# Values of the attention in runs of four key tiles, row sums ahead of the second run, maxima spread anew

## The chip, the cores and the metric

The kernel runs on one core of a Trainium2 chip. Its engines are TensorE (PE in the profile, PEld for its weight loads), VectorE (DVE), ScalarE (ACT), GpSimd (POOL) and SyncE (SP, which here only issues transfers). They run side by side, each through its own list of instructions, and meet at semaphores. The metric is the time of the whole program on the device in microseconds (us), as the median of several runs.

## The reference

Two layers over x, 16 batches of 1024 nodes with 256 channels, each with a residual and a layer norm. The change touches the attention of the first one:

```python
g = relu(einsum('bcn,bnm->bcm', fea, adj * A_s) * para)     # q, from a weighted adjacency
q = g.T in 4 heads of 64;  k, v = (x @ kv_w) in 4 heads of 64
attn = softmax(einsum('bhnd,bhmd->bhnm', q, k) * scale, axis=-1)
out = einsum('bhnm,bhmd->bhnd', attn, v)
x = layernorm(x + out)
```

The second layer aggregates over the adjacency and has two linear layers with batch norms. It comes after the first and is not touched.

## The kernel before

`attention_layer` goes through 16 batches (`over_batches`: batch 0, a loop for 1 to 14, batch 15). In a batch TensorE first does `g_product` (96 matmuls into `sc_ps`), then the products for k and v with the maxima of head 0 between them, and then the four heads.

Scores are computed transposed: a *tile* of 128 keys against 1024 queries, so a head has 8 tiles. Each tile takes two pieces of 512 queries, and each piece two matmuls into the same place of `sc_ps` (L834): one of `qa`, `ka` and one of `qb`, `kb`. The low parts of q lie in `qb`, and with them one row with the negative maximum of every query. So the first `qb` matmul of a head can't begin before that row has arrived. ACT takes the exponential of a whole tile (L378) into `probs`, a ring of 4 tiles. `sc_ps` has two places, so tile i waits for the exponential of tile i-2.

The *values* of a tile (L850) multiply `probs` by v into `pv_ps`; the profile counts 4 matmuls a tile. They free the tile's place in `probs`. In code, tiles come in 4 pairs p = 0 to 3. The values of a pair follow after the scores of the next one, the last pair's after pair 0 of the next head. I call values that stand together a *run*.

The *maxima* of head h+1 are made during head h: 16 *halves* (8 query tiles times two pieces of 512 keys), each one matmul (L803) into one of the two banks of `mx_ps` and one DVE reduction (L562). `MAX_HALVES[h][p][k]` says how many halves stand ahead of unit k of pair p, the last number how many behind the last unit; a unit is the work on a piece (in pair 0, on the parts of a tile). When all 16 are reduced and merged (L566), TensorE transposes the result (L812), DVE negates it into `row` (L573), and SP sends it into `qb` (L192, `store_row`). The next head waits for it (`row_in`).

The *row sums* of head h-1: POOL adds the first seven tiles in six additions (L303), DVE the last one (`add_last`, L579). TensorE sums over the partitions (`sum_up`, L860), ACT copies the result out (`den_copy`, L392), TensorE transposes it (`transpose_sums`, L868), and DVE inverts it (`invert_sums`, L585). The head's output goes by ACT (`head_copy`, L386), TensorE (`transpose_back`, L876) and DVE (`add_head`, L597) into `res`.

During head 3, `prepare` does the first steps of the next batch: TensorE transposes x in two halves (L714, pairs 0 and 1) and makes the k product behind the scores of pair 2 (L698); ACT copies xT_high (L315), DVE makes xT_low (L513). ACT has in its list, behind the exponentials of each pair, also w_high (L338), distance (L325), tanh (L332) and the k copies (L343). In head 0 it normalises the previous batch (L398) behind pairs 0 and 1.

## Time and profile before

| | us |
|---|---|
| median of 3 runs | 2834.18 (2833.53 to 2835.38) |
| the profiled run | 2833.73 |
| its span in the trace | 2831.4 |
| TensorE busy | 2694.5 (95%) |
| DVE busy | 1993.4 (70%) |
| ACT busy | 1668.6 (59%) |
| POOL busy | 1284.4 (45%) |

The attention layer lies between about 20 and 1951 us of the span. Start times in the timeline are counted from the start of the span. Starts of matmuls are measured, their ends are modelled: in a stream of matmuls one is shown as busy for 0.39 us although the next starts 0.23 us later, so a short wait of TensorE can hide in its busy time. The distance from start to start tells more.

### The profile page before, as it was taken

What the parts mean: (1) busy time and instruction counts of PE and PEld (TensorE: products, weight loads), DVE (VectorE), ACT (ScalarE), POOL (GpSimd) and SP (SyncE); (2) the same over time, 40 slices, a digit from 0 to 9 for tenths busy, and PEclk for the clock granted to TensorE, in tenths of its full rate; (3) what the DMA queues carried; (4) which work ended last, traced back from release to release, by engine and by line L of the source; (5) the groups of instructions that cost most, each with busy time, mean ns of one, the idle gap of its engine ahead of it and who ended that gap; (6) DMA issues with size and microseconds to landing.
All of it is one profiled execution on the core that took longest, in us unless ns stands there. A gap on an engine that the chain in (4) does not pass through costs nothing. (4 is left out here: it accounts for less than half of the span.)

```text
span 2831.4 us, 39434 instructions
## 1 busy us (share of the span) xinstructions
PE 2694.5 (95%) x12436; PEld 1857.6 (66%) x12436; DVE 1993.4 (70%) x2875; ACT 1668.6 (59%) x2162; POOL 1284.4 (45%) x684
## 2 busy tenths in 40 slices
PE   7999999999999999999999999996799999989964
PEld 5565665656656566675666756563688888878854
DVE  6687786877878788796887868773533333348878
ACT  7567576765767666676675767654322222237768
POOL 3755657566475754757557575655100000000025
PEclk9999999999999999999999999998899999999976
DMA  4232222233222332222322222222222223215566
GB/s 138 60 94 94 74 67 85 71 100 89 67 71 78 100 93 67 74 78 74 98 88 74 67 85 76 83 65 87 77 90 89 95 104 112 89 30 185 185 237 253
DMA packets 126943, 272.01 MB, mean 96 GB/s; under 512 B 11952, under 2 KB 62128, under 8 KB 123312
## 3 DMA queue, kind: packets, MB, share of 16 engines
q1 hardware_dynamic: 126896, 271.42, 29.7%
q8 instruction: 25, 0.41, 0.1%
q14 instruction: 22, 0.18, 0.0%
HBM read 178.79 MB, written 62.98 MB: 85 GB/s over the span
## 5 line engine op out<-in xcount | busy, mean ns | idle before, releaser
L303 POOL TENSOR_TENSOR psum<-psum,probs 128x1024 f32<-128x1024 f32 x320 | 784.9, 2453 | 144.2 <-ACT probs L378 118.2
L378 ACT ACTIVATE probs<-sc_ps 128x1024 f32<-128x1024 f32 x512 | 508.7, 1024 | 410.0 <-PE sc_ps L834 360.6
L562 DVE TENSOR_REDUCE mx<-mx_ps 128x1 f32<-128x512 f32 x768 | 519.7, 690 | 276.0 <-PE mx_ps L803 274.1
L850 PE MATMUL pv_ps<-probs,v 128*64 128x512 f32 x2048 | 492.4, 604 | 0.0
L834 PE MATMUL sc_ps<-qa,ka 128*128 128x512 f32 x1024 | 387.0, 403 | 0.0
L834 PE MATMUL sc_ps<-qb,kb 128*128 128x512 f32 x1024 | 380.8, 395 | 0.4
L803 PE MATMUL mx_ps<-ka,qa 128*128 128x512 f32 x768 | 315.9, 425 | 10.1 <-DVE mx L562 2.9
L850 PEld LDWEIGHTS pv_ps<-probs,v 128*64 128x64 f32 x2048 | 125.6, 136 | 224.8 <-issue 194.1
L1184 DVE TENSOR_TENSOR agg_lo<-ag_ps,agg_hi 128x1024 fp32r<-128x1024 f32 x32 | 39.2, 1225 | 312.0 <-ACT agg_hi L1111 312.0
L803 PEld LDWEIGHTS mx_ps<-ka,qa 128*128 128x128 f32 x768 | 139.7, 187 | 179.8 <-issue 77.9
L834 PEld LDWEIGHTS sc_ps<-qa,ka 128*128 128x128 f32 x1024 | 187.6, 188 | 105.3 <-issue 64.1
L1080 POOL TENSOR_TENSOR rstd<-veps,neg_half_b 128x4 f32<-128x4 f32 x1 | 1.0, 1007 | 515.9 <-DVE veps L1200 515.9
L526 DVE TENSOR_TENSOR w_lo<-scr,w_hi 128x1024 fp32r<-128x1024 f32 x128 | 224.0, 1750 | 5.3 <-ACT w_hi L338 5.1
L521 DVE SCALAR_TENSOR_TENSOR scr<-scr,adj_ring 128x1024 f32<-128x1024 f32 x128 | 222.8, 1741 | 3.8 <-ACT scr L332 2.8
L834 PEld LDWEIGHTS sc_ps<-qb,kb 128*128 128x128 f32 x1024 | 191.0, 188 | 47.3 <-issue 6.0
L303 POOL TENSOR_TENSOR psum<-probs 128x1024 f32<-128x1024 f32 x64 | 152.5, 2383 | 148.7 <-ACT probs L378 148.6
L1111 ACT ACTIVATE agg_hi<-ag_ps 128x1024 fp32r<-128x1024 f32 x32 | 32.9, 1029 | 311.7 <-PE ag_ps L1272 300.6
L767 PE MATMUL sc_ps<-w_hi,x_hi 128*128 128x512 f32 x512 | 207.1, 405 | 6.8 <-DVE w_lo L526 6.8
L767 PE MATMUL sc_ps<-w_lo,x_hi 128*128 128x512 f32 x512 | 200.6, 392 | 0.0
L767 PE MATMUL sc_ps<-w_hi,x_lo 128*128 128x512 f32 x512 | 200.0, 391 | 0.0
L267 POOL TENSOR_TENSOR rstd<-veps,neg_half 128x8 f32<-128x8 f32 x16 | 32.4, 2025 | 349.5 <-DVE veps L52 349.5
L283 POOL TENSOR_TENSOR qb<-scr,qa 64x1024 fp32r<-64x1024 f32 x64 | 153.4, 2396 | 74.1 <-ACT scr L360 69.2
(197 smaller groups left out, 5554.3 us busy)
## 6 DMA issues: line engine op xcount, KB each, us to landing
adj_ring<-in_adj_dram SPq DMA_DIRECT2D x128, 512.0 KB, 3.7
pre_scratch<-pre SPq DMA_DIRECT2D x28, 1024.0 KB, 4.5
pre<-pre_scratch SPq DMA_DIRECT2D x28, 1024.0 KB, 4.9
x<-in_x_dram SPq DMA_DIRECT2D x16, 1024.0 KB, 5.6
kb<-ka SPq DMA_DIRECT2D x64, 256.0 KB, 3.1
res<-in_x_dram SPq DMA_DIRECT2D x16, 1024.0 KB, 5.6
x_scratch<-res SPq DMA_DIRECT2D x16, 1024.0 KB, 4.5
x1s<-x_scratch SPq DMA_DIRECT2D x16, 1024.0 KB, 7.5
```

The lines of the kernel that those rows point to most:

```text
L283: pool.tensor_tensor(qb[h][own(h), :], scr[own(h), h // 2, :], qa[h][own(h), :].bitcast(F32), ALU.subtract).then_inc(s["ql_done"], 1)
L303: pool.tensor_tensor(psum[:, h % 2, :], probs[:, 0, :] if k == 1 else psum[:, h % 2, :], probs[:, k % PR, :], ALU.add).then_inc(s["pool_ad ...
L378: nc.scalar.activation(probs[:, i % PR, :], sc_ps[:, t % 2, :], ACT.Exp, scale=SCALE)\
L521: nc.vector.scalar_tensor_tensor(d, d, -1.0, adj_ring[:, n % AR, :], ALU.add, ALU.mult)\
L526: nc.vector.tensor_tensor(w_lo[:, n % WR, :], scr[:, n % DR, :], w_hi[:, n % WR, :].bitcast(F32), ALU.subtract).then_inc(s["wlo_done"], 1)
L562: nc.vector.tensor_reduce(mx2[:, nh, n:n + 1], mx_ps[:, nh, :], AX.X, ALU.max)\
L767: ins = nc.tensor.matmul(sc_ps[:, c, cols], lhsT, rhs, start=n == 0 and k == 0, stop=n == T - 1 and k == 2)
L803: nc.tensor.matmul(out, qa[h][:, n * P:(n + 1) * P], ka[h][:, nh * BANK:(nh + 1) * BANK], start=True, stop=True).then_inc(s["mx_ready"], 1)
L834: ins = nc.tensor.matmul(sc_ps[:, t % 2, cols], k[:, keys], q[:, cols], start=part == 0, stop=part == 1)
L850: ins = nc.tensor.matmul(pv_ps[nh * HD:(nh + 1) * HD, h % 2, :], v[:, i, h * HD:(h + 1) * HD], probs[:, i % PR, nh * BANK:(nh + 1) * BANK] ...
L1111: nc.scalar.activation(agg_hi[:, :, j * BANK:(j + 1) * BANK], ag_ps[:, j, :, :], ACT.Copy)\
L1184: nc.vector.tensor_tensor(agg_lo[:, :, cols], ag_ps[:, j, :, :], agg_hi[:, :, cols].bitcast(F32), ALU.subtract)\
```

## The change

The values of a head now come in two runs of four tiles. The first run (tiles 0 to 3) stands behind the scores of pair 2, the second (tiles 4 to 7) behind the scores of pair 0 of the next head, for head 3 at the end of the batch. `sum_up` of the previous head moves from pair 1 to pair 2, directly ahead of the first run, `transpose_sums` directly behind that run, and `transpose_back` stays in pair 3, where no values follow any more. ACT's `den_copy` stays behind pair 1, DVE's `add_last` moves from behind two maxima halves to behind four. `MAX_HALVES` is written anew: no unit has two halves ahead of it except at the start of head 0; head 0 has six halves in pair 2 and three in pair 3, heads 1 and 2 have 4, 5, 5 and 2 (before 4, 4, 6 and 2). No work is added or removed.

```diff
--- before.py
+++ after.py
@@ -65,9 +65,10 @@
     SG = P // 4
     SN = N // 4
     SQ = SN // P
-    MAX_HALVES = [[[0, 2, 1], [2, 1, 1, 1, 0], [2, 1, 1, 1, 1], [1, 1, 0, 0, 0]]] + \
-        2 * [[[0, 1, 1, 1, 1], [1, 1, 1, 1, 0], [2, 1, 1, 1, 1], [1, 1, 0, 0, 0]]]
-    SUM_PAIR, DEN_PAIR, BACK_PAIR = 1, 2, 3
+    MAX_HALVES = [[[0, 2, 1], [0, 1, 1, 1, 1], [1, 1, 1, 1, 2], [1, 1, 1, 0, 0]]] + \
+        2 * [[[0, 1, 1, 1, 1], [1, 1, 1, 1, 1], [1, 1, 1, 1, 1], [1, 1, 0, 0, 0]]]
+    OLD_PAIR, NEW_PAIR = 0, 2
+    GROUP = T // 2
     POOL_ADDS = T - 2
 
     x_v = x.rearrange("b (p t) c -> b p t c", t=T)
@@ -472,7 +473,7 @@
                             prepare(b + 1, h, p)
                         if h and p == 0:
                             head_copy(b, h - 1)
-                        if h and p == SUM_PAIR:
+                        if h and p == NEW_PAIR - 1:
                             den_copy(b, h - 1)
 
             x_high(0, range(T))
@@ -641,10 +642,9 @@
                 maxima_row(b, 1)
 
                 for h in (1, 2):
-                    maxima(b, h + 1, range(0, 1))
+                    maxima(b, h + 1, range(0, 2))
                     add_last(b, h - 1)
-                    maxima(b, h + 1, range(1, 4))
-                    maxima(b, h + 1, range(4, 7))
+                    maxima(b, h + 1, range(2, 7))
                     invert_sums(b, h - 1)
                     maxima(b, h + 1, range(7, T))
                     maxima_row(b, h + 1)
@@ -919,24 +919,24 @@
                             maxes(p, k)
                             scores(b, h, n, parts, part_halves)
                         maxes(p, len(units))
-                        if h and p == DEN_PAIR:
-                            transpose_sums(b, h - 1)
                         if more and p == PAIRS - 1:
                             transpose_maxima(b, h + 1)
-                        if h and p == BACK_PAIR:
+                        if h and p == PAIRS - 1:
                             transpose_back(b, h - 1)
                         if not last:
                             prepare(b + 1, h, p)
-                        if h and p == SUM_PAIR:
-                            sum_up(b, h - 1)
-                        if p:
-                            values(b, h, i - 2)
-                            values(b, h, i - 1)
-                        elif h:
-                            values(b, h - 1, T - 2)
-                            values(b, h - 1, T - 1)
-                values(b, HEADS - 1, T - 2)
-                values(b, HEADS - 1, T - 1)
+                        if h and p == OLD_PAIR:
+                            for n in range(GROUP, T):
+                                values(b, h - 1, n)
+                        if p == NEW_PAIR:
+                            if h:
+                                sum_up(b, h - 1)
+                            for n in range(GROUP):
+                                values(b, h, n)
+                            if h:
+                                transpose_sums(b, h - 1)
+                for n in range(GROUP, T):
+                    values(b, HEADS - 1, n)
 
             pe.wait_ge(s["ident_set"], 3)
             transpose_x(0, 0)
```

How this moves TensorE's list, first at the end of head 1 and the start of head 2 (`ka2`, `qa2` belong to head 2, `ka3`, `qa3` to the maxima of head 3). Before:

```order
L812 MATMUL mx_ps<-ident,mxs 8x128 [waits merged]
L876 MATMUL pv_ps<-ident,heads_t 128x128 [waits rden_done]
L876 MATMUL pv_ps<-ident,heads_t 128x128 x3
L850 MATMUL pv_ps<-probs,v 64x512 [waits exp_done]
L850 MATMUL pv_ps<-probs,v 64x512
L850 MATMUL pv_ps<-probs,v 64x512 [waits exp_done]
L850 MATMUL pv_ps<-probs,v 64x512
L834 MATMUL sc_ps<-qa2,ka2 128x512 [waits kl_done,qa_in2,exp_done]
L834 MATMUL sc_ps<-qa2,ka2 128x512
```

The same place now, down to the first `qb` matmul:

```order
L812 MATMUL mx_ps<-ident,mxs 8x128 [waits merged]
L876 MATMUL pv_ps<-ident,heads_t 128x128 [waits rden_done]
L876 MATMUL pv_ps<-ident,heads_t 128x128 x3
L834 MATMUL sc_ps<-qa2,ka2 128x512 [waits kl_done,qa_in2,exp_done]
L834 MATMUL sc_ps<-qa2,ka2 128x512
L803 MATMUL mx_ps<-ka3,qa3 128x512 [waits kl_done,qa_in3,row_done]
L834 MATMUL sc_ps<-qa2,ka2 128x512 [waits exp_done]
L834 MATMUL sc_ps<-qa2,ka2 128x512
L803 MATMUL mx_ps<-ka3,qa3 128x512
L834 MATMUL sc_ps<-qb2,kb0 128x512 [waits ql_done,kb_in0,row_in]
```

The values of two tiles between the transposes and the scores have gone behind the scores of pair 0; the rest of the order is the same in both.

Second, TensorE in head 3 from the second half of the x transposes (L714) to the k product (L698). Before:

```order
L714 MATMUL mx_ps<-ident,x32 128x128 x7
L860 MATMUL pv_ps<-psum,ones_a 32x256 [waits copied_out,acc_done]
L860 MATMUL pv_ps<-psum,ones_a 32x256 x3
L850 MATMUL pv_ps<-probs,v 64x512 [waits res_added,exp_done]
...
L834 MATMUL sc_ps<-qa3,ka3 128x512 [waits exp_done]
...
L868 MATMUL pv_ps<-ident,heads_t 128x128 [waits den_copied]
L868 MATMUL pv_ps<-ident,heads_t 128x128
L698 MATMUL mx_ps<-xT_hi,kvw_hi 128x512 [waits row_done,xtl_done]
```

Now:

```order
L714 MATMUL mx_ps<-ident,x32 128x128 x7
L834 MATMUL sc_ps<-qa3,ka3 128x512 [waits exp_done]
...
L834 MATMUL sc_ps<-qa3,ka3 128x512 [waits exp_done]
...
L698 MATMUL mx_ps<-xT_hi,kvw_hi 128x512 [waits row_done,xtl_done]
```

Only the scores of pair 2, eight matmuls, are left between them. The row sums, the values and the sums' transposes have moved behind the k product.

## Rows read from the trace of the kernel before

**Rows 1.** Busy time by stretch: engines with their instruction counts, granted clock, DMA share, GB/s

```profile
core 0: us, PE busy (x) PEld busy (x) DVE busy (x) ACT busy (x) POOL busy (x), PEclk, DMA share, GB/s
50.00:1950.00 1900.00, 1887.73 (x8905) 1194.80 (x8904) 1504.26 (x2260) 1268.54 (x1596) 1193.49 (x493) 1.00 0.26 78
```

**Rows 2.** The page's costliest groups: busy us, mean ns of one, idle before, releaser

```profile
L303 POOL TENSOR_TENSOR psum<-psum,probs 128x1024 f32<-128x1024 f32 x320 | 784.9, 2453 | 144.2 <-ACT probs L378 118.2
...
L562 DVE TENSOR_REDUCE mx<-mx_ps 128x1 f32<-128x512 f32 x768 | 519.7, 690 | 276.0 <-PE mx_ps L803 274.1
```

**Rows 3.** Timeline (start us, us, engine, line): runs of two tiles, of four; head copy

```profile
1910.44 0.40 PE L803 MATMUL mx_ps<-ka,qa 128*128 128x512 f32 x1
1910.77 1.94 PE L850 MATMUL pv_ps<-probs,v 128*64 128x512 f32 x8
1912.64 0.50 PE L803 MATMUL mx_ps<-ka,qa 128*128 128x512 f32 x1
1912.97 0.39 PE L834 MATMUL sc_ps<-qa,ka 128*128 128x512 f32 x1
...
1915.28 0.39 PE L834 MATMUL sc_ps<-qb,kb 128*128 128x512 f32 x1
...
1912.75 0.60 ACT L386 ACTIVATE heads_t<-pv_ps 128x512 f32<-128x512 f32 x1 [0.87 <-PE pv_ps L850]
...
1828.38 3.65 PE L850 MATMUL pv_ps<-probs,v 128*64 128x512 f32 x16
1831.96 0.50 PE L767 MATMUL sc_ps<-w_hi,x_hi 128*128 128x512 f32 x1
```

**Rows 4.** Timeline, the row's way into head 0: batch 14, then batch 15

```profile
1745.98 0.27 PE L812 MATMUL sc_ps<-ident,mxs 128*8 128x128 f32 x1
...
1746.29 0.28 DVE L573 TENSOR_SCALAR row<-sc_ps 8x128 fp32r<-8x128 f32 x1 [0.37 <-PE sc_ps L812]
...
1746.59 0.70 SPq L192 DMA_DIRECT2D qb<-row  x1
...
1747.52 1.08 PE L834 MATMUL sc_ps<-qa,ka 128*128 128x512 f32 x4
1748.63 0.70 PE L834 MATMUL sc_ps<-qb,kb 128*128 128x512 f32 x2
...
1866.26 0.27 PE L812 MATMUL sc_ps<-ident,mxs 128*8 128x128 f32 x1
...
1866.87 0.70 SPq L192 DMA_DIRECT2D qb<-row  x1
...
1868.72 0.30 PEld L834 LDWEIGHTS sc_ps<-qb,kb 128*128 128x128 f32 x2 [0.27 <-DMA qb<-row]
```

**Rows 5.** Timeline of TensorE, batch 14: sums' transposes; end of head 1 to head 2

```profile
1780.69 0.38 PE L868 MATMUL pv_ps<-ident,heads_t 128*128 128x128 f32 x2
1781.00 1.94 PE L850 MATMUL pv_ps<-probs,v 128*64 128x512 f32 x8
...
1785.27 0.27 PE L812 MATMUL mx_ps<-ident,mxs 128*8 128x128 f32 x1
...
1789.27 0.63 PE L834 MATMUL sc_ps<-qb,kb 128*128 128x512 f32 x2
```

**Rows 6.** Timeline, head 0 of batch 14: an exponential; head 1 begins

```profile
1753.48 1.03 ACT L378 ACTIVATE probs<-sc_ps 128x1024 f32<-128x1024 f32 x1
...
1766.65 0.73 PE L834 MATMUL sc_ps<-qa,ka 128*128 128x512 f32 x2
```

**Rows 7.** Timeline, head 3 of batch 14: x transposes, xT_low, exponentials, k product

```profile
1815.60 1.03 PE L714 MATMUL mx_ps<-ident,x 128*128 128x128 f32 x8
...
1821.10 0.47 PE L698 MATMUL mx_ps<-xT_hi,kvw_hi 128*128 128x512 f32 x1
...
1817.85 1.23 DVE L513 TENSOR_TENSOR xT_lo<-mx_ps,xT_hi 128x1024 fp32r<-128x1024 f32 x1 [1.72 <-ACT xT_hi L315]
...
1820.32 1.95 ACT L378 ACTIVATE probs<-sc_ps 128x1024 f32<-128x1024 f32 x2 [1.28 <-PE sc_ps L834]
...
1827.31 1.94 ACT L378 ACTIVATE probs<-sc_ps 128x1024 f32<-128x1024 f32 x2
```

**Rows 8.** Busy time by stretch, the end of the attention layer; columns as in rows 1

```profile
1947.00:1951.00 4.00, 1.97 (x17) 0.71 (x14) 1.43 (x2) 0.98 (x2) 0.39 (x1) 1.00 0.00 0
```

## The prediction

> **What bounds the kernel now.** First the busy time by stretch: from 50 to 1950 us, the attention layer, TensorE is busy 1887.7 of 1900 us at a granted clock of 1.00, its full 2.4 GHz, while ACT, DVE and POOL have 21 to 37% to spare [rows 1]. Nothing is changed behind it. So the question is how long TensorE's own list of work takes there, and where it begins to wait. A batch takes 120.3 us: the same transfer is issued at 1746.59 and 1866.87 [rows 4].
>
> Second, TensorE's timeline around a run of values. Ten 512-column matmuls for scores and maxima in a row take 2.31 us (1912.97 to 1915.28) [rows 3]; I use 0.232 each. A run of two tiles lasts 1.87 us to the next work, a run of four 3.58, so two more tiles cost 1.71, and 0.16 belongs to the run as such. The matmul ahead of it holds 0.33 instead of 0.23 (1910.44 to 1910.77), the one behind it too (1912.64 to 1912.97). **A run costs 0.10 + 0.16 + 0.10 = 0.36 us whatever its length** [rows 3].
>
> Third, what a run hides. Between heads the maxima are transposed (L812), DVE negates them (L573), SP sends the row to `qb` (L192), and the next head's first `qb` matmul waits for it. Into head 0 no run lies between, and the wait shows. In batch 14: transpose 1745.98, DVE 1746.29, transfer 1746.59, `qb` matmul 1748.63, which is 1.11 us behind the first of four `qa` matmuls that fill 0.93. In batch 15 the weight load stood 0.27 us for this very transfer, 1.85 us from issue to use [rows 4]. The whole chain is thus 2.65 us in a loop batch (14 batches alike) and 2.46 in batch 15. Into heads 1 to 3 a run covers it: from 1785.27 to the `qb` matmul at 1789.27 there are 4.00 us [rows 5].
>
> **The change, part by part.**
>
> *Fewer runs.* Before, a batch has 3 runs in head 0 and 4 in each other head, the last pair of tiles already joined to one: 15. Now there are 8. Seven times 0.36 is 2.52 us. The back transposes now stand without a run behind them. Two transposes ahead of a run take 0.31 where 0.22 is their own (1780.69 to 1781.00 [rows 5]), so an entry is worth 0.09; alone they cost between nothing and that. I give back 0.1 a batch: **2.4 us saved**.
>
> *The row transfer loses its cover.* No run stands behind L812 at the three inner boundaries. What is left ahead of the first `qb` matmul: L812 0.11, four back transposes 0.44 (not into head 1), four `qa` matmuls 0.93, two maxima halves 0.46 (not into head 3). That is 1.51, 1.95 and 1.48 us against a chain of 2.64. **Waits of 1.13, 0.69 and 1.16, sum 3.0 us**; with 2.46 the sum is 2.4. I take 2.64, the row of the loop batches, for 14 of the 16. A wait for the exponential of tile 7, some 0.2 us at the second `qa` pair, falls inside these. Behind TensorE nothing is late: the exponentials of tiles 0 and 1 wait for buffers until the next run anyway.
>
> *Maxima spread.* DVE takes 0.69 us a half [rows 2] and has two buffers, so one half with two score matmuls (0.70) is just carried, and halves side by side are not. Head 0 before: 18.02 us (1748.63 [rows 4] to 1766.65 [rows 6]) for 44 matmuls of 0.232, three runs of 2.07 and L812, 16.55 in all: waits of 1.47. Head 0 now: 0.25 at the third half, 0.24 where two halves meet between pairs 1 and 2. Then tile 4 waits for the exponential of tile 2, as no run stands ahead of it: that one begins at 1753.48, behind four normalisations [rows 6], and ends at 1754.51, where TensorE stands ready at 1753.8 by my walk: 0.74. Then 0.25 at the doubled half, and 0.22 because L812 follows its last half more closely. Together 1.7, **0.2 worse**. In heads 1 and 2 one wait of 0.25 moves from behind a run to between the pairs and stays. DVE adds the last tile two halves later; its reader, now behind pair 2, is later still.
>
> *Exponentials behind a run of four.* Those of tiles 4 and 5 now wait until the values of tiles 0 and 1 free their buffers. ACT sees a run of two end 1.98 us after its start (1910.77 to 1912.75 [rows 3]), one tile so 0.855 earlier, after 1.12. In heads 1 and 2 they end 2.1 and 3.1 us into a run of 3.58: free. POOL's six additions (2.45 us each [rows 2]) end some 3.4 us behind L812, ahead of what needs them.
>
> *Head 3, where the next batch is prepared.* Count from R, the start of its first run. Exponentials 0 and 1 end at R+3.1 (freed tile by tile). ACT then has xT_high, w_high and head_copy until R+5.4, exponentials 2 and 3 until R+7.4, and xT_high of the second half until R+8.3; DVE's xT_low takes 1.23 [rows 7], until R+9.6. TensorE comes to its k product at R+8.5: only two score tiles lie between the second x transposes and it, where there were 5.5 us (1815.60 to 1821.10 [rows 7]). **1.2 there, and 0.2 before it for exponential 2.** Behind exponentials 4 and 5 ACT has w_high, distance, tanh and two k copies, so exponential 6 begins 7.0 us after exponential 4 (1820.32, 1827.31 [rows 7]). Exponential 4 now starts 1.1 into TensorE's next run, so 6 ends 9.1 into it. TensorE needs it after 3.58 (run) + 0.3 (transposes of the sums) + 1.86 (scores) + 0.54 (back transposes) + 1.71 (values 4 and 5) = 8.0. **1.1, and 0.2 in all around tile 7.** Before, it ended at 1828.33, just ahead of a run that began at 1828.38 [rows 3]. Head 3 together 2.7 us. The ends: with ACT free the k product would still wait 0.5, so 1.5 in all; and if TensorE needs, at each stop inside the loop, the 0.18 by which 2.03 differs from 1.85 in rows 4, it is 3.2.
>
> **The sum.** Middle batch: −2.4 + 0.2 + 3.0 + 2.7 = +3.5 us, times 14 = +49. Batch 0 has the shorter chain and no normalisations (0.4 less): −2.4 − 0.4 + 2.4 + 2.7 = +2.3. Batch 15 prepares nothing, and its tail hangs on POOL's chain from exponential 1, 0.4 later: +0.5. Total +51.8. The profiled run took 2833.73 us, its span 2831.4, and the run is 0.45 under the median of three: **2885.5 us**.
>
> **The rivals.**
> A, forecast: row waits and head 3's waits both stand: 2885.
> B: only the row waits stand. For it, ACT's spare time; against, its fixed order, which in head 3 left exponential 6 no idle time before it [rows 7]. Then −2.4 + 0.2 + 3.0 = +0.8 a batch: 2846.
> C, faster: the handovers are quicker than I read. All added waits, 5.7 us in a middle batch, are what chains have over the matmuls beside them: the row chain three times, ACT's two in head 3. The change wins once these five are together 3.5 us shorter, 0.7 each; with none left, −2.2 × 16 = −35: 2799. The row chain would need 1.9 us, where its rows show 2.46 and 2.65. The Trainium skill, DMA: Bandwidth & Descriptors (its split of a transfer into a fixed and a variable cost), gives about 2.0 us for any small transfer, which would leave a row of 4 KB no way to come sooner; the 1.85 and 2.04 from issue to use agree.
> D: the waits cancel the gain, 2834; it takes 2.2 us of them in place of 5.7.
> E: TensorE's clock falls to 1.2 GHz after the new idle times of about 1 us. From 1947 to 1951 it is busy 1.97 of 4 us in pieces, and the granted clock stays 1.00 [rows 8], so it should not. If it did for 3 us of every batch, 1.5 us of work would be lost each time: 2909. The Trainium skill, TensorE: Matmul & The Clock Gate (Part 1), has the clock halved by an idle stretch; by it, this case would come about only if stops as short as these counted as one.
>
> **How the numbers follow.** A 0.66, B 0.17, C 0.09, D 0.05, E 0.03. A alone spans 2862 (1.5 us in head 3, the short chain) to 2900 (3.2, and 0.18 at each stop). The range takes in B: **2843 to 2902**. A measurement of this kernel can tell about 0.2%, 5.7 us, from no change. Faster 0.09, same 0.05, slower 0.86.
>
> **What would show it.** Runs of 3.6 us, 128 of them, all of four tiles. L812 to `qb` matmul 2.6 us at the inner boundaries, with a wait for `qb<-row`. In head 3 a wait for xT_low ahead of L698 and one for an exponential inside the last run. Batches of 123.8 us. I am wrong if the `qb` matmul comes 2.0 us behind L812, or if head 3 shows no wait over 0.3 us.

## The result

The changed kernel takes 2886.24 us (median of 4 runs, 2885.2 to 2888.24) against 2834.23 for the kernel before (4 runs, 2833.53 to 2835.38): a ratio of 1.0184, 95% interval 1.0171 to 1.0196. It is 52.0 us slower, where 51.8 was forecast. The profiled run took 2886.49 us, its span 2884.1. TensorE's granted clock is 1.00 from 50 to 2000 us, as it was from 50 to 1950 us before (rows 1), so nothing of this is the clock.

The page of the kernel after: busy time of the engines, then from its costliest groups one line: the busy us, the mean ns of one, and the idle time before it with its releaser. Lines have moved by one behind the first edit (the exponential is L379, the row's transfer L193).

```profile
PE 2694.8 (93%) x12436; PEld 1851.4 (64%) x12436; DVE 1953.8 (68%) x2875; ACT 1663.5 (58%) x2162; POOL 1276.0 (44%) x684
...
L850 PE MATMUL pv_ps<-probs,v 128*64 128x512 f32 x2048 | 471.9, 600 | 17.3 <-ACT probs L379 17.3
```

TensorE's busy time is what it was (2694.5 before), and its idle time grew by 52.4 us. That doesn't mean that the runs that went saved nothing. The value matmuls (L850) are shown busy for 20.5 us less than before (492.4), and the start of each wait hides in the modelled end of the matmul ahead of it, so that busy time grew elsewhere. What a run and a wait are worth is read from start to start, below. The waits that the profile shows, added up over the program (us in total, times, longest):

```profile
PE pv_ps L850 <- ACT probs L379: 17.3, 15, 1.2
PE mx_ps L698 <- DVE xT_lo L514: 17.0, 16, 2.5
PE sc_ps L834 <- DMA qb<-row: 16.6, 47, 0.8
```

These are the three waits that the prediction named: an exponential inside head 3's last run (15 batches), xT_low ahead of the k product, and the row, at 47 of the 48 inner boundaries. Together 51 us, of which 2.5 (the longest of the second row, ahead of the first k product) were there before.

Batch 14 begins and ends with the transpose of head 0's maxima, 123.73 us apart (120.28 before, by rows 4). Timeline, as start us, length, engine, line; first that transpose, then a run of four (it answers to rows 3), then the boundary from head 0 to head 1 and the one from head 2 to head 3 (rows 5 before):

```profile
1794.03 0.27 PE L812 MATMUL sc_ps<-ident,mxs 128*8 128x128 f32 x1
...
1917.76 0.27 PE L812 MATMUL sc_ps<-ident,mxs 128*8 128x128 f32 x1
...
1827.31 3.65 PE L850 MATMUL pv_ps<-probs,v 128*64 128x512 f32 x16
1830.89 0.44 PE L868 MATMUL pv_ps<-ident,heads_t 128*128 128x128 f32 x2
...
1812.48 0.27 PE L812 MATMUL mx_ps<-ident,mxs 128*8 128x128 f32 x1
...
1812.80 0.28 DVE L574 TENSOR_SCALAR row<-mx_ps 8x128 fp32r<-8x128 f32 x1 [0.37 <-PE mx_ps L812]
...
1813.10 0.69 SPq L193 DMA_DIRECT2D qb<-row  x1
...
1814.95 0.73 PE L834 MATMUL sc_ps<-qb,kb 128*128 128x512 f32 x2 [0.37 <-DMA qb<-row]
...
1854.61 0.27 PE L812 MATMUL mx_ps<-ident,mxs 128*8 128x128 f32 x1
...
1855.97 0.73 PE L834 MATMUL sc_ps<-qa,ka 128*128 128x512 f32 x2 [0.18 <-ACT probs L379]
1857.07 1.19 PE L834 MATMUL sc_ps<-qb,kb 128*128 128x512 f32 x4 [0.36 <-DMA qb<-row]
```

The run of four lasts 3.58 us to the next work, as read before the change. From L812 to the first `qb` matmul it is 2.47 us (1812.48 to 1814.95), 2.66 into head 2 and 2.46 (1854.61 to 1857.07) into head 3. Into head 2 the `qb` matmul now comes 2.66 us behind L812, where rows 5 had 4.00 with a run between.

Head 3 of the same batch: DVE's second xT_low and the k product; then ACT's exponentials 4 and 5, its two k copies, exponentials 6 and 7; then TensorE's last run, which answers to rows 3 and 7.

```profile
1867.39 1.23 DVE L514 TENSOR_TENSOR xT_lo<-mx_ps,xT_hi 128x1024 fp32r<-128x1024 f32 x1 [1.56 <-ACT xT_hi L316]
...
1868.67 0.50 PE L698 MATMUL mx_ps<-xT_hi,kvw_hi 128*128 128x512 f32 x1 [0.97 <-DVE xT_lo L514]
1869.01 0.39 PE L698 MATMUL mx_ps<-xT_hi,kvw_lo 128*128 128x512 f32 x1
...
1873.46 1.94 ACT L379 ACTIVATE probs<-sc_ps 128x1024 f32<-128x1024 f32 x2 [0.74 <-PE pv_ps L850]
...
1878.38 2.04 ACT L344 ACTIVATE ka<-mx_ps 64x1024 fp32r<-64x1024 f32 x2
1880.44 1.94 ACT L379 ACTIVATE probs<-sc_ps 128x1024 f32<-128x1024 f32 x2
...
1878.43 1.94 PE L850 MATMUL pv_ps<-probs,v 128*64 128x512 f32 x8
1881.52 2.00 PE L850 MATMUL pv_ps<-probs,v 128*64 128x512 f32 x8 [1.16 <-ACT probs L379]
```

The k product stands 0.97 us for xT_low. The last run stops after tiles 4 and 5, 1.38 us longer than its eight matmuls take (3.09 from start to start, 1.71 of work), because exponential 6 begins at 1880.44. Exponential 4 had waited for the values of tile 0 to free its place in `probs`.

A batch splits at TensorE's transposes of maxima (L812) and at its first G matmul (L767). The stretches of batch 14 in us, the same in the kernel before and after; the next column adds up the prediction's terms of that stretch (runs that go, by 0.36 each, and waits):

| stretch | before | after | difference | by the prediction |
|---|---|---|---|---|
| head 0, L812 to L812 | 18.60 | 18.45 | -0.15 | -0.36 + 0.2 = -0.16 |
| head 1 | 20.69 | 20.99 | +0.30 | -0.72 + 1.13 = +0.41 |
| head 2 | 21.09 | 21.14 | +0.05 | -0.72 + 0.69 = -0.03 |
| head 3, L812 to L767 | 25.60 | 28.84 | +3.24 | -0.72 + 1.16 + 2.7 = +3.14 |
| G, k and v products | 34.30 | 34.31 | 0 | 0 |
| batch | 120.28 | 123.73 | +3.45 | +3.5 with 0.1 given back |

The loss lies in head 3. In heads 0 to 2 the waits are about paid by the runs that went.

### The profile page after: what moved, and what is told of

It reads as the page before. It is cut to its first block and busy times, and to the rows that moved or that the text cites. A ratio compares the mean times of both kernels' runs of the same rounds, so it can differ in the third digit from the quotient of the medians.

```text
span 2884.1 us, 39434 instructions
## 1 busy us (share of the span) xinstructions
PE 2694.8 (93%) x12436; PEld 1851.4 (64%) x12436; DVE 1953.8 (68%) x2875; ACT 1663.5 (58%) x2162; POOL 1276.0 (44%) x684
## 5 line engine op out<-in xcount | busy, mean ns | idle before, releaser
L304 POOL TENSOR_TENSOR psum<-psum,probs 128x1024 f32<-128x1024 f32 x320 | 775.5, 2423 | 204.5 <-ACT probs L379 175.5
L379 ACT ACTIVATE probs<-sc_ps 128x1024 f32<-128x1024 f32 x512 | 503.4, 1024 | 368.8 <-PE pv_ps L850 180.0
L850 PE MATMUL pv_ps<-probs,v 128*64 128x512 f32 x2048 | 471.9, 600 | 17.3 <-ACT probs L379 17.3
L834 PE MATMUL sc_ps<-qa,ka 128*128 128x512 f32 x1024 | 395.1, 409 | 5.7 <-ACT probs L379 4.7
L850 PEld LDWEIGHTS pv_ps<-probs,v 128*64 128x64 f32 x2048 | 132.9, 136 | 283.8 <-issue 238.3
L522 DVE SCALAR_TENSOR_TENSOR scr<-scr,adj_ring 128x1024 f32<-128x1024 f32 x128 | 228.6, 1786 | 25.7 <-ACT scr L333 25.3
L767 PE MATMUL sc_ps<-w_hi,x_hi 128*128 128x512 f32 x512 | 207.1, 404 | 7.3 <-DVE w_lo L527 7.3
L767 PE MATMUL sc_ps<-w_lo,x_hi 128*128 128x512 f32 x512 | 200.5, 392 | 0.0
L767 PE MATMUL sc_ps<-w_hi,x_lo 128*128 128x512 f32 x512 | 200.0, 391 | 0.0
L1272 PE MATMUL ag_ps<-a_hi,x_hi 128*128 128x512 f32 x480 | 186.8, 389 | 0.0
L1272 PE MATMUL ag_ps<-a_hi,x_lo 128*128 128x512 f32 x480 | 186.8, 389 | 0.0
L1272 PE MATMUL ag_ps<-a_lo,x_hi 128*128 128x512 f32 x480 | 186.7, 389 | 0.0
```

The costliest lines, as they stand in the source:

```text
L304: pool.tensor_tensor(psum[:, h % 2, :], probs[:, 0, :] if k == 1 else psum[:, h % 2, :], probs[:, k % PR, :], ALU.add).then_inc(s["pool_ad ...
L379: nc.scalar.activation(probs[:, i % PR, :], sc_ps[:, t % 2, :], ACT.Exp, scale=SCALE)\
L522: nc.vector.scalar_tensor_tensor(d, d, -1.0, adj_ring[:, n % AR, :], ALU.add, ALU.mult)\
L767: ins = nc.tensor.matmul(sc_ps[:, c, cols], lhsT, rhs, start=n == 0 and k == 0, stop=n == T - 1 and k == 2)
L834: ins = nc.tensor.matmul(sc_ps[:, t % 2, cols], k[:, keys], q[:, cols], start=part == 0, stop=part == 1)
L850: ins = nc.tensor.matmul(pv_ps[nh * HD:(nh + 1) * HD, h % 2, :], v[:, i, h * HD:(h + 1) * HD], probs[:, i % PR, nh * BANK:(nh + 1) * BANK] ...
```

## Experiments

The theory under test is that of the prediction: runs cost 0.36 us each whatever their length; what they used to cover (the row, the handovers of head 3) comes out as waits. A second theory would have the long run itself at fault, for instance by the ring of four places that it fills and empties. The stretches of a middle batch, from the same marks as above:

| kernel | head 0 | head 1 | head 2 | head 3 | G | batch | median us |
|---|---|---|---|---|---|---|---|
| before | 18.60 | 20.69 | 21.09 | 25.60 | 34.30 | 120.28 | 2834.8 |
| after | 18.45 | 20.99 | 21.14 | 28.84 | 34.31 | 123.73 | 2886.2 |
| e1_no_row_wait | 18.43 | 20.30 | 21.18 | 28.23 | 34.29 | 122.43 | 2866.1 |
| e3_k_product_late | 18.46 | 20.98 | 21.15 | 27.55 | 34.29 | 122.43 | 2868.6 |
| e6_k_late_reciprocal_early | 18.46 | 20.98 | 21.15 | 26.20 | 34.86 | 121.65 | 2854.7 |
| e11_after_ring_of_8 | 18.44 | 20.94 | 21.15 | 27.45 | 34.31 | 122.29 | 2865.4 |
| e4_maxima_only | 18.05 | 20.86 | 20.72 | 25.61 | 34.30 | 119.54 | 2822.8 |
| e7_maxima_add_later | 17.97 | 20.22 | 20.69 | 25.62 | 34.30 | 118.80 | 2812.6 |
| e10_maxima_tuned | 18.58 | 20.22 | 20.69 | 25.61 | 34.30 | 119.40 | 2822.2 |
| e9_runs_of_one | 19.92 | 21.70 | 22.13 | 26.16 | 34.29 | 124.20 | 2897.9 |
| e8_one_joined_run | 18.27 | 20.62 | 20.68 | 25.18 | 35.19 | 119.94 | 2828.0 |
| e12_joined_run_with_maxima | 19.14 | 20.18 | 20.60 | 25.21 | 35.13 | 120.26 | 2834.3 |
| e5_covered_runs | 16.30 | 20.96 | 21.40 | 27.85 | 34.29 | 120.80 | 2842.8 |

In e5 the values of two tiles (1.71 us of work) lie in head 3's stretch instead of head 0's, in e9 those of one tile (0.855) in head 0's instead of head 3's. The kernel before ran beside all of them, at 2833.9 to 2835.0.

### The row

The row of maxima of heads 1 to 3 goes to a spare tile, by the same transfer, and TensorE waits for its arrival in head 0 alone. So the maxima are not subtracted in three of the four heads.

```diff
+                target = sink[:, :] if h else qb[h][r:r + 1, :].rearrange("o (t p) -> o t p", p=P)
+                sp.dma_start(target.bitcast(F32),
...
                 if 1 in parts and 0 in halves and i == 0:
-                    wait(pe, s["row_in"], 16 * (4 * b + h + 1))
+                    if h == 0:
+                        wait(pe, s["row_in"], 16 * (4 * b + 1))
```

> The changed kernel, but the maxima row of heads 1 to 3 is sent to a spare tile in place of qb, and TensorE doesn't wait for it (these heads' scores lack their maxima; the transfers are as many and as large). Theory: the three waits for the row cost 2.65 us a middle batch and 0.1 of restart each; 0.75 of it is hidden behind, a wait for the exponential of tile 7 which then shows. So -2.1 us a batch, -34 in all: 2852 us. Rival, the exponentials and POOL's additions set the pace there anyway and the row is only what is seen last: the time stays at 2880 or more.

Measured: 2866.08 us (4 runs), ratio 1.011 (1.0094 to 1.0127), 20 us less than after. That lies between what the two theories gave. Head 1 won 0.69 us and head 3 0.61, but head 2 nothing. There TensorE waits for something else now (DVE, then TensorE):

```profile
1816.29 1.63 DVE L601 SCALAR_TENSOR_TENSOR res<-pv_ps,rden,res 128x64 f32<-128x64 f32 x8 [0.27 <-PE pv_ps L880]
1817.83 2.67 DVE L566 TENSOR_REDUCE mx<-mx_ps 128x1 f32<-128x512 f32 x4
...
1818.57 0.50 PE L806 MATMUL mx_ps<-ka,qa 128*128 128x512 f32 x1 [0.29 <-DVE mx L566]
```

DVE is still adding head 0's output (L601) when the first halves of the next maxima come, and has reduced none of them until 1818.5. So taking the row out saves the change 1.3 us a batch (20 us over 16 batches), not the 2.65 by which its three chains exceed the matmuls beside them: behind the row wait stand others, the exponential of tile 7 and DVE's additions.

The same edit on the kernel before:

> The same edit on the kernel before. Both theories: a run of values covers the row there, so 2834 within 3 us. If it falls by more, the edit itself does something else and e1 can't be read as the row's price.

Measured: 2834.43 us, ratio 0.9998 (0.9988 to 1.0007). With runs of two behind L812, the row costs nothing at the inner boundaries. It is the run that hides it.

### Head 3

The k product moves behind the scores of pair 3, ACT's k copies behind exponentials 6 and 7.

```diff
                     tanh_half(b, 3)
+                if (h, p) == (3, 3):
                     k_high(b, 0)
                     k_high(b, 1)
...
-                if (h, p) == (3, 2):
+                if (h, p) == (3, 3):
                     k_product(b)
```

> The changed kernel with the k product of the next batch behind the scores of pair 3, and ACT's two k copies behind exponentials 6 and 7. Theory: in head 3 the wait for xT_low (1.13 and 0.1 of restart) and the one for exponential 6 (1.44) go: -2.7 us in each of 15 batches, -40: 2846 us. Rival, the two waits only move, to the end of head 3 or into g_product, because ACT and DVE have the same work to do in the same time: less than half of it, 2866 or more.

Measured: 2868.57 us (4 runs), ratio 1.0117 (1.01 to 1.0134). The rival was nearer. Both waits of head 3 are gone from the trace, which shows their cause, but of the 2.7 us a batch that were expected 1.3 came, and the rest went into a new wait. DVE, POOL and TensorE in head 3:

```profile
1851.65 3.17 DVE L523 SCALAR_TENSOR_TENSOR scr<-scr,adj_ring 128x1024 f32<-128x1024 f32 x1
1854.75 3.42 DVE L528 TENSOR_TENSOR w_lo<-scr,w_hi 128x1024 fp32r<-128x1024 f32 x1
1858.09 0.20 DVE L587 RECIPROCAL rden<-pv_ps 128x8 f32<-128x8 f32 x1
...
1851.38 2.36 POOL L304 TENSOR_TENSOR psum<-psum,probs 128x1024 f32<-128x1024 f32 x1 [0.16 <-POOL psum L304]
1853.90 3.19 POOL L304 TENSOR_TENSOR psum<-psum,probs 128x1024 f32<-128x1024 f32 x1 [0.16 <-POOL psum L304]
...
1854.90 0.44 PE L869 MATMUL pv_ps<-ident,heads_t 128*128 128x128 f32 x2
...
1858.35 0.65 PE L877 MATMUL pv_ps<-ident,heads_t 128*128 128x128 f32 x4 [1.16 <-DVE rden L587]
```

The transposed sums are there at 1855.3, but the reciprocal stands in DVE's list behind w_low, which takes 3.42 us because POOL adds beside it. The next kernel takes the reciprocal ahead of that w_low:

```diff
                     weigh(b + 1, 2)
-                    w_low(b + 1, 1)
                 invert_sums(b, 2)
                 if not last:
+                    w_low(b + 1, 1)
                     w_low(b + 1, 2)
```

> The changed kernel with the k product behind pair 3 of head 3 as in e3_k_product_late, and VectorE's reciprocal of head 2's sums taken ahead of w_low of tile 1 instead of behind it, since TensorE's back transposes waited 1.16 us for rden there. Theory (that wait was only VectorE's order): 1.2 to 1.3 us less a batch than e3_k_product_late, about 2849 us. Rival (the adjacency rows and VectorE's slowed passes set when head 3 can end, and the wait moves on to the next batch's G or to the k product): 2862 us or more.

Measured: 2854.72 us (4 runs), ratio 1.0072 (1.0056 to 1.0089), between the 2849 of the theory and the 2862 of the rival. Head 3 fell by 1.35 us to 26.20, as the theory had it, and 0.57 came back in the next batch's G, as the rival had it. There TensorE wants the row sums of head 3:

```profile
1857.50 1.22 DVE L581 TENSOR_TENSOR psum<-psum,probs 128x1024 f32<-128x1024 f32 x1
...
1858.77 0.64 PE L861 MATMUL pv_ps<-psum,ones_a 128*32 128x256 f32 x8 [0.51 <-DVE psum L581]
```

DVE now does in a shorter head 3 the same work at the same slowed pace, and stands 0.57 us for the transposed sums ahead of the reciprocal. Its addition ends 32.4 us behind head 3's L812, as in e3, while TensorE asks for the sums 1.35 us earlier. With e6 the change has lost 2.1 us a batch of its waits and is still 0.7% slower than the kernel before.

The other suspect for the last run is the ring. Eight places instead of four; memory is made by letting the low parts of x and of the weights share the tiles of the high parts, and by holding one half of `neg_para`. So the values computed are others, the instructions the same.

```diff
-    WR, DR, AR, PR = 3, 3, 2, 4
+    WR, DR, AR, PR = 3, 3, 2, 8
...
-        x_lo = sb("x_lo", [P, T, C], F32R)
+        x_lo = x_hi
```

> The changed kernel with eight buffers for the exponentials (probs) instead of four, so that no exponential waits for the values of four tiles before. Memory for them is made by leaving things out: the low parts of x and of the weights share the tiles of the high parts, and neg_para holds one of its two halves; its instructions stay the same in number and shape. Theory (the wait for exponential 6 inside head 3's last run, 1.16 us, comes from exponentials 4 and 5 that had to wait for a buffer until the run of tiles 0 to 3): it falls to 0.2 and 1.2 us a batch go, about 2867 us; the small waits for the exponential of tile 7 go too, but the wait for the row takes their place. Rival (ScalarE's fixed order with two k copies ahead of exponential 6 sets it, whatever the buffers): 2880 us or more.

Measured: 2865.43 us (4 runs), ratio 1.0106 (1.0089 to 1.0123), 20.8 us less than after; 19 were expected. ACT and TensorE in head 3:

```profile
1852.18 1.94 ACT L377 ACTIVATE probs<-sc_ps 128x1024 f32<-128x1024 f32 x2
1859.16 1.94 ACT L377 ACTIVATE probs<-sc_ps 128x1024 f32<-128x1024 f32 x2
...
1857.99 1.94 PE L848 MATMUL pv_ps<-probs,v 128*64 128x512 f32 x8
1860.24 1.08 PE L848 MATMUL pv_ps<-probs,v 128*64 128x512 f32 x4 [0.31 <-ACT probs L377]
```

From exponential 4 to 6 there are still 6.98 us (1852.18 to 1859.16; 1873.46 to 1880.44 in the changed kernel), all of them ACT's list. But 4 needs no place from the run any more. It starts behind ACT's copy of the row sums, earlier against TensorE's list, and the wait falls from 1.16 to 0.31. So the wait in the last run is the product of two things, the late start by the ring and ACT's list of 7 us behind it. Taking away either removes most of it (e11 the ring, e3 the list). The wait for xT_low fell from 0.97 to 0.66 us.

### What a run costs

> e7_maxima_add_later with every run of two value tiles cut into two runs of one: the first of them now stands between the pair's two score tiles, the second where the run stood. 32 runs a batch instead of 15, nothing else moved. It prices a run in the other direction. Theory (0.36 us for each run, whatever its length): 17 x 0.36 = 6.1 us more a batch, 98 in all, about 2911 us. Rival (switching is cheaper than read, and the row of a run of two told of something that lay behind it, such as a buffer): under 2870 us. If the first of the two runs must also wait for its exponential the time goes above 2911, and the trace names it.

```diff
                         for k, (n, parts, part_halves) in enumerate(units):
+                            if k == len(units) // 2:
+                                if p:
+                                    values(b, h, i - 2)
+                                elif h:
+                                    values(b, h - 1, T - 2)
...
-                            values(b, h, i - 2)
                             values(b, h, i - 1)
```

Measured: 2897.92 us (4 runs), ratio 1.0222 (1.0205 to 1.0239), 85.3 more than e7. The text on record counts 32 runs; there are 30, since the last three tiles of head 3 stay together, so 15 more and not 17. Then 85.3 / 16 / 15 = 0.355 us a run. TensorE's timeline shows the same:

```profile
1824.38 0.62 PE L834 MATMUL sc_ps<-qa,ka 128*128 128x512 f32 x2
1824.94 1.08 PE L850 MATMUL pv_ps<-probs,v 128*64 128x512 f32 x4
1825.95 0.50 PE L803 MATMUL mx_ps<-ka,qa 128*128 128x512 f32 x1
1826.29 0.63 PE L834 MATMUL sc_ps<-qb,kb 128*128 128x512 f32 x2
```

A run of one takes 1.01 us to the next work, where its tile is worth 0.855; the matmul behind it holds 0.34 instead of 0.23, the two ahead 0.56 instead of 0.46. The price of 0.36 holds for runs of one, two and four tiles.

### The maxima

The kernel before with nothing but the new `MAX_HALVES`:

```diff
-    MAX_HALVES = [[[0, 2, 1], [2, 1, 1, 1, 0], [2, 1, 1, 1, 1], [1, 1, 0, 0, 0]]] + \
-        2 * [[[0, 1, 1, 1, 1], [1, 1, 1, 1, 0], [2, 1, 1, 1, 1], [1, 1, 0, 0, 0]]]
+    MAX_HALVES = [[[0, 2, 1], [0, 1, 1, 1, 1], [1, 1, 1, 1, 2], [1, 1, 1, 0, 0]]] + \
+        2 * [[[0, 1, 1, 1, 1], [1, 1, 1, 1, 1], [1, 1, 1, 1, 1], [1, 1, 0, 0, 0]]]
```

> The kernel before with the new table of maxima alone, values still in runs of two. Theory (two buffers, 0.69 us a half): in heads 1 and 2 no two halves meet any more without a run between, -0.25 each; in head 0 waits of some 0.9 in place of 1.47. Together -1.0 us a batch, -16: 2818 us. Rival, the spread pays only with runs of four, and DVE's adding of the last tile, now among more halves, takes it back: 2831 to 2837.

Measured: 2822.75 us (4 runs), ratio 0.9955 (0.9939 to 0.9972). This part of the change alone is a gain of 12 us, for which the theory gave 16. Heads 0 and 2 fell by 0.55 and 0.37 us, head 1 rose by 0.17. There DVE's addition of the last tile waits for POOL behind two halves, and the third half with it. DVE and TensorE of e4, then DVE at the same place of e7, where the addition comes behind four halves:

```profile
1760.65 1.23 DVE L579 TENSOR_TENSOR psum<-psum,probs 128x1024 f32<-128x1024 f32 x1 [1.19 <-POOL psum L303]
...
1762.53 0.50 PE L803 MATMUL mx_ps<-ka,qa 128*128 128x512 f32 x1 [0.57 <-DVE mx L562]
```

```profile
1748.31 2.75 DVE L562 TENSOR_REDUCE mx<-mx_ps 128x1 f32<-128x512 f32 x4 [2.48 <-PE mx_ps L803]
1750.98 1.22 DVE L579 TENSOR_TENSOR psum<-psum,probs 128x1024 f32<-128x1024 f32 x1
```

The edit, on top of e4:

```diff
-                    maxima(b, h + 1, range(0, 1))
+                    maxima(b, h + 1, range(0, 2))
                     add_last(b, h - 1)
-                    maxima(b, h + 1, range(1, 4))
+                    maxima(b, h + 1, range(2, 4))
```

> e4_maxima_only (the kernel before with the spread of maxima of the change, runs of two) with VectorE's addition to the sums behind the first four halves of a head's maxima instead of behind two, since in head 1 it waited for GpSimd's sum and held TensorE 0.57 us at the third half. Theory (a mere place in VectorE's order): 0.7 us less a batch, about 2812 us. Rival (the addition comes too late for the row sums behind pair 2, or the halves wait elsewhere): 2823 us or more.

Measured: 2812.64 us (4 runs), ratio 0.9922 (0.9905 to 0.9938). Both edits are in the change, and the kernel after differs from e7 only in its runs of four and in where the steps of the row sums stand beside them. So these cost 2886.2 - 2812.6 = 73.6 us, 4.93 a batch (0.48 in head 0, 0.77, 0.45 and 3.22 in the others), and the small edits hid 22 of them. e7 is the best of all versions here.

One more step by the same trace:

```diff
-    MAX_HALVES = [[[0, 2, 1], [0, 1, 1, 1, 1], [1, 1, 1, 1, 2], [1, 1, 1, 0, 0]]] + \
+    MAX_HALVES = [[[1, 1, 1], [0, 1, 1, 1, 1], [2, 1, 1, 1, 1], [2, 1, 0, 0, 0]]] + \
```

> e7_maxima_add_later with its maxima moved once more by what its trace shows: in head 0 one half ahead of the first qb matmul, no two halves side by side except behind a run of values, and the last halves directly behind the run, so that the transposed maxima follow three tiles of scores later as in head 1. Theory (halves side by side without a run ahead of them cost 0.25 to 0.45 us each, and the transpose 0.24 when it follows its last half closely): 0.7 us less a batch, about 2801 us. Rival (head 0 is held by the exponential behind the normalisations, and the wait moves there): 2810 us or more.

Measured: 2822.22 us (4 runs), ratio 0.9955 (0.9939 to 0.9972): the rival, 10 us slower than e7. TensorE in head 0:

```profile
1738.06 0.50 PE L803 MATMUL mx_ps<-ka,qa 128*128 128x512 f32 x1 [0.20 <-ACT v L364]
...
1740.34 0.50 PE L834 MATMUL sc_ps<-qa,ka 128*128 128x512 f32 x1 [0.38 <-ACT probs L378]
```

The half ahead of the first `qb` matmul needs the bank that ACT's copy of v still reads; it delays the scores of tiles 0 and 1, their exponentials, and so the scores of tile 2.

### Long runs with the row covered

If only uncovered waits make the change slow, longer runs in better places should win. Two kernels tried it. The first has 8 runs a batch as the change has, but the four middle tiles lie behind L812. It differs in more than the runs: a spread table of maxima of its own, DVE's addition behind eight halves, `head_copy` behind pair 1, and in head 3 the first x transposes and ACT's two copies of xT_high ahead of a pair's scores and exponentials. The part of the edit with the runs:

```diff
+                        if p == 1:
+                            if h:
+                                values(b, h - 1, T - 2)
+                                values(b, h - 1, T - 1)
+                            values(b, h, 0)
+                            values(b, h, 1)
...
+                        if p == PAIRS - 1:
+                            for n in range(2, T - 2):
+                                values(b, h, n)
```

> The kernel before with as few runs as the change (8 a batch instead of 15), but placed so that every row of maxima keeps matmuls behind its transpose: a run of four tiles (two old, two new) behind pair 1, a run of the middle four behind the transposed row of pair 3, where the row's way through VectorE, SyncE and the queue lies beside it; row sums behind the first of the two, and the spread maxima of the change. Theory (runs are worth 0.36 us each, and the loss of the change is only in uncovered waits): 7 x 0.36 = 2.5 us less a batch, 0.3 given back, so about 2799 us and no wait for qb<-row. Rival (the longer runs themselves delay ScalarE's exps or VectorE's maxima, and new waits eat the gain): 2823 us or more.

Measured: 2842.77 us (8 runs), ratio 1.0026 (1.0015 to 1.0037). The wait for the row is gone (it is in no row of TensorE's waits), and so is all of the gain. Here is TensorE behind L812 of head 1, then in head 3:

```profile
1791.69 3.65 PE L847 MATMUL pv_ps<-probs,v 128*64 128x512 f32 x16
...
1798.59 0.50 PE L831 MATMUL sc_ps<-qa,ka 128*128 128x512 f32 x1 [0.26 <-ACT probs L378]
...
1820.36 0.50 PE L831 MATMUL sc_ps<-qa,ka 128*128 128x512 f32 x1 [0.74 <-ACT probs L378]
```

The second and third lines are the scores of tile 2, which need exponential 0. With no run behind pair 0 they follow at once. In head 3 ACT has the copy of xT_high ahead of that exponential, which this kernel's own edit put there, so that part is not the price of the runs alone. In heads 1 and 2 this is 0.43 us longer than the matmuls take, in head 3 0.89, and with it go 0.35 where two halves now meet ahead of a run and 0.2 where `sum_up` waits for ACT's copy directly behind a run. Before, the run behind pair 0 covered this handover, the run behind pair 1 the halves.

The second keeps the runs behind L812 and behind pair 0 as they are, and joins only those behind pairs 1 and 2 of the kernel before; the k product and the reciprocal lie as in e6.

```diff
-                        if p:
+                        if p == 2:
+                            for n in range(4):
+                                values(b, h, n)
+                            if h:
+                                transpose_sums(b, h - 1)
+                        elif p == 3:
                             values(b, h, i - 2)
```

> The kernel before with only the runs behind pairs 1 and 2 joined to one run of four tiles behind pair 2 (row sums ahead of it, transposed sums behind it; the runs behind pair 3 and behind pair 0 of the next head stay, and so the cover of the row), the spread maxima of the change, the k product behind pair 3 and the reciprocal earlier as in e6. 11 runs a batch instead of 15. Theory: 4 x 0.36 = 1.44 us less a batch for the runs and 0.7 for the maxima, so 2.1 x 16 = 34 us, about 2800 us. Rival (a join in the middle of a head costs ScalarE's exps their slack, as in the changed kernel, whatever stands behind the row): 2820 us or more.

Measured: 2827.99 us (10 runs), ratio 0.9978 (0.9968 to 0.9987). The text on record is wrong in one point: this kernel has the maxima table of the kernel before, and DVE's addition in its old place. So it is to be held against the kernel before alone, and the theory gives 1.44 x 16 = 23 us less, 2812. It kept 7 of the 23. Two of its waits, over the program, name where the rest went; the first stands in each batch's G (+0.89 us), the second in the heads. The first need not be the join's, as the next kernel shows:

```profile
PE pv_ps L861 <- DVE psum L580: 12.8, 16, 1.2
...
PE mx_ps L804 <- DVE mx L563: 7.4, 30, 0.4
```

The last kernel joins the same runs on top of e7's two edits, with a maxima table for this order of runs, the reciprocal ahead of `w_low` as in e6, and TensorE's k product directly behind the joined run:

```diff
+    MAX_HALVES = [[[0, 2, 1], [0, 1, 1, 1, 1], [0, 1, 1, 1, 1], [2, 1, 1, 1, 0]]] + \
+        2 * [[[0, 1, 1, 1, 1], [2, 1, 1, 1, 1], [0, 1, 1, 1, 1], [2, 0, 0, 0, 0]]]
...
                             if h:
                                 transpose_sums(b, h - 1)
+                            if h == 3 and not last:
+                                k_product(b + 1)
```

> A correction first: e8_one_joined_run had the maxima table of the kernel before, and VectorE's addition in its old place, not the spread maxima that its text on record says, so it tells only of the joined run. This kernel joins the runs behind pairs 1 and 2 of a head to one of four tiles behind pair 2, as e8 did, with maxima spread for this order of runs (two halves side by side only behind a run), VectorE's addition behind four halves as in e7, the k product directly behind the joined run and the reciprocal early. 11 runs a batch. Theory (a join costs nothing where row and first scores keep their cover): 4 x 0.36 = 1.44 us less a batch than e7_maxima_add_later, about 2790 us. Rival (the joined run takes slack from ScalarE and VectorE wherever it lies, as e5, e6 and e8 showed it in the row sums, the exponentials and the maxima): 2812 us or more.

Measured: 2834.3 us (10 runs), ratio 1.0001 (0.9992 to 1.0011): the rival, 22 us slower than e7. Against e7, heads 1 and 2 gained 0.04 and 0.09 us and head 3 0.41; head 0 lost 1.17 and G 0.83. TensorE's waits, then DVE in head 3 of batch 14:

```profile
PE pv_ps L860 <- DVE psum L579: 12.0, 15, 1.2
...
PE sc_ps L834 <- ACT probs L378: 11.3, 16, 0.8
...
PE mx_ps L812 <- DVE mxs L566: 8.4, 16, 0.5
...
1823.48 0.21 DVE L585 RECIPROCAL rden<-pv_ps 128x8 f32<-128x8 f32 x1 [2.83 <-PE pv_ps L868]
```

The second and third are head 0's, once in each of the 16 batches: tile 4 again waits for an exponential, as no run stands ahead of it, and the transpose waits for the last halves. The third might be had back by another table, which was not tried; the second is a price of the join. The first is not shown to be one. DVE stands 2.83 us for the transposed sums (as in e8), because in its list both `w_low` come behind the reciprocal, and its last addition ends 31.7 us behind head 3's L812, where it ended 31.0 behind it in e7. The wait in G is in every kernel with this place of the reciprocal (e6, e8, e12) and in no other. No run has the join without it, so how much of the 0.83 to 0.89 us in G belongs to the join stays open.

## Why the prediction was right, and where its terms were off

*Fewer runs, 7 times 0.36 us.* Right. The run of four lasts 3.58 us as read, and e9 prices a run at 0.355 us from the other side. The 0.1 us given back was too small. The waits of the batch (2.65, 2.5 and 1.8 us) less the 1.47 of head 0 before and less 2.52 for the runs make 3.0, against 3.45 measured. By the table of stretches nearly all of the 0.5 us between them lies in head 3 (3.24 measured; 0.98 and 2.5 less 0.72 make 2.8). TensorE's timeline has four pieces of about 0.1 us there that the sum leaves out. The first matmul behind the row wait and behind the k product's wait holds about 0.34 us instead of 0.23 (1868.67 to 1869.01 for the second). The last matmul ahead of `sum_up` (1871.31 to 1871.63) and the first behind the second x transposes (1865.58 to 1865.92) hold 0.32 and 0.34. Before, those transposes and `sum_up` stood side by side ahead of a run. No experiment separates the four.

*Row waits, 3.0 us.* The mechanism is right, by e1 and e2. The chain was 2.47, 2.66 and 2.46 us instead of 2.64 three times, so TensorE stood 0.96, 0.71 and 0.98 us longer than its matmuls, 2.65 in all. What the sum does not tell is what the row alone is worth: the prediction remarked that a wait of 0.2 us for exponential 7 falls inside, and with DVE's additions to `res` what stands behind the row is half of the sum. Without the row, 1.3 us are saved, not 2.65. It made no difference to the total, but would have to any repair.

*Maxima.* Head 0's waits came to 1.82 us where 1.7 was said. The verdict "0.2 worse" (0.35 measured) is right only beside runs of four. There tile 4 waits for the exponential of tile 2, with no run ahead of it. With runs of two the same table gains 0.55 us in head 0 and 0.4 in head 2 (e4). The prediction took the maxima and the runs as separate terms; for head 0 they aren't.

*Head 3, 2.7 us.* The k product: 0.97 us of idle time, 1.13 over its matmuls, for 1.2. The last run: 1.16 idle, 1.38 over its matmuls, for 1.1 and 0.2. The 0.2 for exponential 2 did not show. Together 2.5. e3 and e11 confirm both causes, the second as the ring's and ACT's list together.

*The rivals.* B (only row waits) is out by 17.0 and 17.3 us of head 3's waits. C wanted the five chains 3.5 us a batch shorter, D the added waits at 2.2 us; they were 5.2, and the row's chain was never under 2.45. E: the clock stayed 1.00. From issue to use the row took 1.85 us into head 1 (1813.10 to 1814.95) and head 3, and 2.05 into head 2. The Trainium skill, DMA: Bandwidth & Descriptors (Anatomy of one DMA), has about 2.0 us as the fixed part of a transfer, fitted there to transfers that GpSimd issues. The row is issued by SyncE, and this trace agrees within 0.15.

*The ends.* From its first L812 to the next batch's, batch 0 lost 3.1 us where 2.3 was forecast. Batch 15, from its first L812 to its last value matmul, lost 0.9 where 0.5 was.

That the total was hit to 0.2 us is partly luck. The waits for the row and in head 3 came out 0.35 and 0.2 us a batch below their terms, those of head 0 0.15 above, and the 0.5 us that the sum lacked made up for it. A miss of 0.2 us is also less than the interval of the measurement.

## What to carry to other kernels

A switch of matmul shape has a fixed price that two rows of a timeline give (0.36 us here). But before switches are saved by joining short pieces, list for each piece what handover of another engine it covers: here the four runs of a head covered the row, an exponential, two halves side by side and the row sums, and no join that was tried kept more than a third of its gain, though e5, e8 and e12 carried other edits that may have cost them part of it. When a change bundles edits, run them apart: two of its small ones were worth 22 us, and the large one cost over 70. After a wait is removed, look at what stands right behind it; e1 and e3 got back about half of what the trace put down to the wait, e6 two thirds.

## What the runs showed of the hardware

TensorE pays for a stop beyond the stop itself: behind a wait the first score or k matmul of 512 columns holds 0.31 to 0.34 us instead of 0.23 (86 places in the changed kernel, between 50 and 1950 us), as at the edge of a run.

DVE and POOL slow each other in head 3. In e3, DVE's pass at 1851.65 begins while POOL adds (1851.38 to 1853.74) and ends at 1854.82, 1.08 us behind it; POOL's addition at 1853.90 begins while DVE is at work and takes 3.19 us instead of 2.4; the next DVE pass (1854.75) takes 3.42 instead of 1.2 and ends 1.1 us behind POOL again. They take turns rather than share. The Trainium skill, SBUF — State Buffer (Summary: rules for kernel authors), says that a VectorE operation with two inputs in SBUF and a GpSimd operation that reads SBUF lock each other out, the later one until the earlier has finished; these rows agree. A DVE reduction from PSUM is not slowed: e7's four halves at 1748.31 take 2.75 us, 0.69 each, while POOL adds from 1748.53 to 1750.92.
